# A transformer kernel whose second layer's keys and values are projected ahead of the experts and parked in DRAM

## The reference, cut to what matters

```
x = x + self_output(FFN(...(cross attention on layernorm(x) and ctx, then self attention)))   # 16 heads of 16
x = x + experts(layernorm(x))     # router of 8, top 2 of 7 experts and a no-op, 256 tokens an expert
x = x + mha(layernorm(x), ctx, ctx, W_q, b_q, W_k, b_k, W_v, b_v, W_o, b_o)                   # second layer
x = x + depth_block(layernorm(x)) # the better half of the tokens of a batch through one FFN
```

## Time and profile before

| What | Value |
|---|---|
| Median of 3 runs | 915.57 us (915.12 to 917.22) |
| Profiled execution, its own time | 916.68 us |
| Its span, first to last instruction | 914.9 us |
| TensorE busy | 779.9 us, 85% |
| VectorE busy | 563.6 us, 62% |
| ScalarE busy | 422.9 us, 46% |
| GpSimd busy | 394.8 us, 43% |
| DMA moved | 83.76 MB, mean 92 GB/s |
| Mean granted TensorE clock | 0.933 |

### The profile page before, as it was taken

How to read it: one execution, slowest core, us unless ns; L and a number is a source line. 1 busy time by engine, 2 the same in 40 slices (tenths; PEclk the granted TensorE clock), 3 DMA queues, 4 the chain that set the end, 5 groups by cost and what they waited for, 6 DMA issues and landing times.

```text
span 914.9 us, 16951 instructions
## 1 busy us (share of the span) xinstructions
PE 779.9 (85%) x6606; PEld 632.9 (69%) x6606; DVE 563.6 (62%) x1171; ACT 422.9 (46%) x703; POOL 394.8 (43%) x381
## 2 busy tenths in 40 slices
PE   4778999999999878999962999990677999779897
PEld 4655777777777646999862788880455767558896
DVE  4556887888878663779884002103568998855332
ACT  3134776777767566545610111210125677664132
POOL 7554573443455454635456220007845554242200
PEclk9978999999999999999985899995659999999999
DMA  8966677757785602300051551532775865500011
GB/s 195 173 119 95 118 122 101 107 91 130 115 123 97 82 3 93 117 1 26 27 204 44 180 200 39 89 115 65 129 125 83 117 99 72 71 3 12 13 35 35
DMA packets 58500, 83.76 MB, mean 92 GB/s; under 512 B 8722, under 2 KB 35345, under 8 KB 58372
## 3 DMA queue, kind: packets, MB, share of 16 engines
q1 hardware_dynamic: 55170, 76.47, 43.8%
q0 software_dynamic: 3072, 6.04, 2.8%
q10 hardware_dynamic: 178, 0.16, 0.1%
HBM read 36.74 MB, written 10.11 MB: 51 GB/s over the span
## 4 chain that ended last, share of the span: by engine, by line
PE 66%; DVE 13%; DMA 6%; POOL 5%; issue 4%; ACT 2%; SPq 2%; POOLq 0%; DVEq 0%; ACTq 0%
PE ps L608 8%; PE ps L187 8%; PE ps L672 7%; PE ps L188 6%; PE ps L189 6%; DVE nmax L1290 6%; PE ps L769 6%; PE ps L783 5%; PE ps L630 4%; PE ps L211 3%; PE ps L822 3%; PE ps L832 3%; PE ps L646 2%; POOL moe_in L1149 2%; DMA kst<-k_parts 2%
## 5 line engine op out<-in xcount | busy, mean ns | idle before, releaser
L1290 DVE TENSOR_REDUCE nmax<-ps 128x4 f32<-128x1024 f32 x192 | 234.9, 1224 | 93.2 <-PE ps L608 91.5
L915 ACT ACTIVATE prob<-ps 128x1024 f32<-128x1024 f32 x192 | 196.3, 1022 | 73.1 <-PE ps L630 71.1
L1074 POOL TENSOR_TENSOR rstd<-var,half 128x2 f32<-128x2 f32 x56 | 43.9, 784 | 279.4 <-DVE var L1241 202.3
L608 PE MATMUL ps<-kst,qst 50*128 50x256 f32 (+1 forms) x768 | 100.2, 343 | 32.8 <-DVE nmax L1290 22.6
L608 PEld LDWEIGHTS ps<-kst,qst 50*128 50x128 f32 (+1 forms) x768 | 60.6, 196 | 74.9 <-DVE nmax L1290 43.6
L672 PE MATMUL ps<-prob,vext 128*32 128x256 f32 x1536 | 106.9, 397 | 0.6 <-ACT oext L928 0.6
L630 PE MATMUL ps<-qst,kst 51*128 51x256 f32 (+1 forms) x768 | 81.5, 291 | 15.0 <-ACT prob L915 9.9
L630 PEld LDWEIGHTS ps<-qst,kst 51*128 51x128 f32 (+1 forms) x768 | 60.7, 192 | 21.7 <-ACT prob L915 13.3
L1161 POOL DMA_INDIRECT gat<-moe_out,slu x32 | 35.2, 1101 | 72.8 <-issue 72.8
L672 PEld LDWEIGHTS ps<-prob,vext 128*32 128x32 f32 x1536 | 41.2, 112 | 32.4 <-issue 4.2
L1082 POOL TENSOR_SCALAR hres<-xres,mv,rstd 128x256 f32<-128x256 f32 x48 | 58.9, 1232 | 2.6
(11 more groups left out here) (214 smaller groups left out, 2045.1 us busy)
## 6 DMA issues: line engine op xcount, KB each, us to landing
kst<-k_parts SPq DMA_DIRECT2D x144, 128.0 KB, 5.8
qst<-q_parts SPq DMA_DIRECT2D x144, 128.0 KB, 4.1
e_in<-in_ein SPq DMA_DIRECT2D x5, 1024.0 KB, 5.0
e_out<-in_eout SPq DMA_DIRECT2D x5, 1024.0 KB, 8.8
ctx_raw<-in_ctxT SPq DMA_DIRECT2D x16, 256.0 KB, 6.5
ew_in<-in_ein SPq DMA_DIRECT2D x2, 1024.0 KB, 6.2
ew_out<-in_eout SPq DMA_DIRECT2D x2, 1024.0 KB, 9.7
out<-xres SPq DMA_DIRECT2D x8, 256.0 KB, 2.1
```

Source lines behind the costliest of these rows:

```text
L608: last = pe.matmul(score_pair(n, p)[:, 512 * s + S * t:512 * s + S * (t + 1)], qst[j][a:b, p, t * P:(t + 1) * P], kst[j][a:b, p, :], start ...
L915: act.activation(probs[p % 4][:].rearrange("p i t s -> p (i t s)"), T_PS, ACT.Exp).then_inc(sm["exp_done"], 1)
L1290: dve.tensor_reduce(nmax[n % 2][:, :, :, p].rearrange("p t s -> p s t"), score_pair(n, p).rearrange("p (s t k) -> p s t k", s=2, t=TB), AX ...
```

## The change

K and V of all eight batches of the second layer are projected after the last FC2 and before expert 0 (`park` on TensorE). The contexts are loaded early in the FFN; ACT makes their rounded parts, VectorE the remainders. ACT writes K's rounded part out of PSUM; TensorE subtracts it in PSUM by a product with a negative identity, and ACT writes what is left as the remainder. V is copied out by ACT. Three DMAs per batch store both parts of K (512 KB) and V (256 KB) in DRAM; parts live in the buffers of the exponentials, so batches 4 to 7 wait for the stores of batches 0 to 3. Five DMAs per item (`stack_k`) bring them back later, K straight into the stack, V to a compact buffer (`vc`), from which POOL spreads it into vext (`values`).

The weights of W_k and W_v are split in the FFN (chunks 12 and 13), in buffers of their own. Experts use other buffers (E_BUF), and their first weights are loaded after FC2 of items 6 and 7. T_E0 is 2 later in the plan. In the entry, the combine of batch 1 stands a little later and that of batch 3 ahead of item 16's scores, batch 0's first tile is combined after two gathers, VectorE instead of POOL normalizes items 16 and 17, and the second half of the query stack of items 0 and 16, and of the key stack of item 0, is issued on ACT's queue. The three memsets of key stacks run after experts 2, 4 and 5 (before: 2, 3 and 6), those of vext on POOL. At the start the DMA of the zero mask comes later. Several semaphores are merged.

Core of the diff, sixteen leading blanks cut where there are as many. In order: constants and buffers; SP (park_load, park_store, stack_k, expert_weights, expert_tokens); TensorE's park; ACT's second_half and park and its wait before an expert's relu; POOL's values and attention; VectorE's second_stacks, queries, park and combine.

```diff
-T_E0 = T_F0 + F_STEP * (B - 1) + 54
+T_E0 = T_F0 + F_STEP * (B - 1) + 56
...
+    k_park = nc.dram_tensor("k_park", [B, 2, 2, P // 2, TB * S], F32, kind="Internal").ap()
+    v_park = nc.dram_tensor("v_park", [B, P, TB * D], F32, kind="Internal").ap()
...
-        SET = [n % 4 for n in range(12)] + [0, 1, 2, 0] + [n % 3 for n in range(NA, 3 * B)]
+        SET = [n % 4 for n in range(12)] + [0, 1, 2, 0] + [(n - NA) % 3 for n in range(NA, 3 * B)]
...
+        PARK_CTX = ((c_hi[1], c_lo[1]), (aT_hi, aT_lo),
+    *((t[0][:, 4 * i:4 * i + 2, :], t[0][:, 4 * i + 2:4 * i + 4, :]) for t in (qst, kst) for i in range(2)),
+    (hT_hi, hT_lo), (c_hi[0], c_lo[0]))
+        PARK_V = [vext[1 + i // 2][:].rearrange("p t h e -> p (t h e)")[:, i % 2 * TB * D:(i % 2 + 1) * TB * D] for i in range(4)]
...
+        PARK_K = (22.6, 24.4, 28.6, 32, 36.4, 38.9, 44, 46)
+        PARK_AT = dict(c_hi=(-77, -69, -64, -56, -51, -43, -4, 8.5), c_lo=(-76, -67.5, -63, -54.5, -50, -41.5, -2.5, 10.5))
+        PARK_STEP = dict(k=0, v=0.7, k_lo=1.5, k_hi=0.9, v_out=1.7, k_low=1.9, store=2.5)
...
-        E_BUF = [0, 3, 1, 2, 0, 3, 0]
+        E_BUF = [1, 2, 0, 3, 1, 2, 3]
...
+def park_load(b):
+    yield T_F0 + 5 if b < 4 else park_at(b - 4, "c_lo") + 2
+    if b == 0:
+        sp.wait_ge(sm["ctx_ready"], B)
+        sp.wait_ge(sm["oT_ps"], 2 * NA)
+    elif b == 2:
+        sp.wait_ge(sm["pv_ps"], 4 * NA)
+    elif b >= 4:
+        sp.wait_ge(sm["ctx_ready"], B + b - 3)
+    sp.dma_start(raw_ctx(b), ctxT[b].rearrange("(k p) s -> p k s", p=P)).then_inc(sm[ctx_sem(b)], 16)
+def park_store(b):
+    n = NA + b
+    yield park_at(b, "store") if b < 6 else T_E0 - 3.2 + 0.1 * b
+    sp.wait_ge(sm["k_split"], n + 1)
+    for c in range(2):
+        sp.dma_start(k_park[b, :, c], park_k(b)[:, c].bitcast(F32)).then_inc(sm[f"park{b % 4}"], 16)
+    sp.wait_ge(sm["park_s"], b + 1)
+    sp.dma_start(v_park[b], PARK_V[b % 4]).then_inc(sm[f"park{b % 4}"], 16)
...
+    if n >= NA:
+        yield expert_start((3, 5, 6)[n - NA]) + 4 if n < NA + 3 else start_of(n) - 6.7
+        if n < NA + NSET:
+            sp.wait_ge(sm["kst_one"], n - NA + 1)
+        else:
+            sp.wait_ge(sm["st_ps"], HG * (last_user(n) + 1))
+        if n == NA:
+            for i in range(4):
+                sp.wait_ge(sm[f"park{i}"], 96)
+            sp.wait_ge(sm["y_ready"], 1)
+        elif n >= NA + 2:
+            sp.wait_ge(sm["v_ready"], n - 1)
+        for s in range(2):
+            sp.dma_start(kst[j][64 * s:64 * s + 2 * DH].rearrange("p h s -> p (h s)").bitcast(F32),
+                         k_park[n - NA, s].rearrange("c (d q) x -> (c d) (q x)", q=4)).then_inc(sm[f"stk_k{j}"], 16)
+            sp.dma_start(kst[j][64 * s + 2 * DH:64 * s + 3 * DH].rearrange("p h s -> p (h s)").bitcast(F32),
+                         k_park[n - NA, s, 0].rearrange("(d q) x -> d (q x)", q=4)).then_inc(sm[f"stk_k{j}"], 16)
+        sp.dma_start(v_compact(n), v_park[n - NA]).then_inc(sm[f"stk_k{j}"], 16)
+        return
...
-    yield (T_F0 + 2, T_F0 + 10, ffn_start(7) + 13, ffn_start(7) + 27, *(expert_start(k) + 7.5 for k in (0, 1, 4)))[e]
-    if e == 0:
-        sp.wait_ge(sm["st_ps"], HG * NA)
-    elif e == 1:
-        sp.wait_ge(sm["op_ps"], NA)
+    yield (ffn_start(7) + 10, ffn_start(7) + 23, T_E0 - 2, T_E0 + 5.5, *(expert_start(k) + 7.5 for k in (1, 2, 3)))[e]
+    if e < 2:
+        sp.wait_ge(sm["fc2_ps"], B - 1 + e)
     elif e < 4:
-        sp.wait_ge(sm["fc2_ps"], e + 5)
-    else:
-        sp.wait_ge(sm["efc2_ps"], (0, 1, 4)[e - 4] + 1)
+        sp.wait_ge(sm["v_ps"], NA + B)
+    else:
+        sp.wait_ge(sm["efc2_ps"], e - 2)
...
-    yield expert_start(e) - (4 if e < 2 else 8)
+    yield expert_start(e) - 4 if e == 0 else expert_start(e) - 4.5 if e == 1 else expert_start(e) - 8
     if e == 0:
         sp.wait_ge(sm["scat"], 16 * 2 * NT)
         sp.wait_ge(sm["x_add"], B)
+        sp.wait_ge(sm["park_lo"], B)
...
+def park(b):
+    n, src = NA + b, PARK_CTX[b]
+    k_dst, v_dst = park_banks(b)
+    yield park_at(b, "k")
+    pe.wait_ge(sm["ctx_ready"], B + b + 1)
+    if b == 0:
+        pe.wait_ge(sm["w_lo_s"], 14)
+        pe.wait_ge(sm["gelu"], KF * B)
+    if b >= 2:
+        pe.wait_ge(sm["k_split"], n - 1)
+    for m in range(KD):
+        for k in range(KD):
+            last = mm3(pe, k_dst[m], [v[:, k, m * P:(m + 1) * P] for v in W[2][1]], [v[:, k, :] for v in src], k == 0, k == KD - 1)
+    last.then_inc(sm["k_ps"], 1)
+    yield park_at(b, "v")
+    if b == 2:
+        pe.wait_ge(sm["fres_s"], B)
+    elif b:
+        pe.wait_ge(sm["park_s"], max(b - 1, 1))
+    pe_project(pe, v_dst, W[2][2], src).then_inc(sm["v_ps"], 1)
+    yield park_at(b, "k_lo")
+    pe.wait_ge(sm["k_hi_s"], n + 1)
+    if b == 0:
+        pe.wait_ge(sm["nident_s"], 1)
+    for m in range(KD):
+        last = pe.matmul(k_dst[m], nident[:], park_k(b)[:, 0, m, :], start=False, stop=True, skip_group_check=True)
+    last.then_inc(sm["park_lo"], 1)
...
+def second_half(n, which, at):
+    yield at
+    act.wait_ge(sm[f"{which}_split"], n + 1)
+    if n:
+        act.wait_ge(sm["kst_one"], n - NA + 1)
+    else:
+        act.wait_ge(sm["init_d"], 2)
+    dst = (qst if which == "q" else kst)[SET[n]]
+    for c in range(3):
+        act.dma_start(dst[64 + DH * c:64 + DH * (c + 1), :, :].bitcast(F32), PARTS[which][c][64:128, :, :].bitcast(F32)).then_inc(sm[f"stk_{which}{SET[n]}"], 16)
...
+def park(b):
+    n = NA + b
+    yield park_at(b, "c_hi")
+    act.wait_ge(sm[ctx_sem(b)], 16 * (b // 4 + 1 + (0 if b % 4 else B)))
+    if b >= 6:
+        act.wait_ge(sm["fc1_ps"], KF // 2 * (b + 1))
+    elif b == 2:
+        act.wait_ge(sm["st_ps"], HG * NA)
+    elif b == 1:
+        act.wait_ge(sm["op_ps"], NA)
+    act.activation(PARK_CTX[b][0][:], raw_ctx(b), ACT.Copy).then_inc(sm["ctx_hi_s"], 1)
+    yield park_at(b, "k_hi")
+    act.wait_ge(sm["k_ps"], n + 1)
+    if b >= 4:
+        act.wait_ge(sm[f"park{b % 4}"], 48)
+    else:
+        act.wait_ge(sm["hid_ready"], 2 * (B - 1) + b // 2 * 2)
+    for m in range(KD):
+        last = act.activation(park_k(b)[:, 0, m, :], park_banks(b)[0][m], ACT.Identity, bias=cols[:, 5, m:m + 1])
+    last.then_inc(sm["k_hi_s"], 1)
+    yield park_at(b, "v_out")
+    act.wait_ge(sm["v_ps"], n + 1)
+    act.activation(PARK_V[b % 4], park_banks(b)[1], ACT.Copy).then_inc(sm["park_s"], 1)
+    yield park_at(b, "k_low")
+    act.wait_ge(sm["park_lo"], b + 1)
+    for m in range(KD):
+        last = act.activation(park_k(b)[:, 1, m, :], park_banks(b)[0][m], ACT.Identity, bias=cols[:, 5, m:m + 1])
+    last.then_inc(sm["k_split"], 1)
...
+            act.wait_ge(sm[f"park{2 * e + i}"], 96)
...
+def values(n):
+    j = n % VSET
+    if n < NA + VSET:
+        yield T_E0 + 15 + n - NA if j else T_C0 + 9
+        if j:
+            for i in range(2):
+                gp.wait_ge(sm[f"park{2 * (j - 1) + i}"], 96)
+        else:
+            gp.wait_ge(sm["st_y0"], 16 * 4)
+            gp.wait_ge(sm["st_y1"], 16 * 3)
+        ch(gp.memset(vext[j][:], 1.0))
+    yield T_E0 + 34 + 12 * (n - NA) if n < NA + 2 else start_of(n) + 2.5
+    gp.wait_ge(sm[f"stk_k{SET[n]}"], stk_k_count(n))
+    if n >= NA + VSET:
+        gp.wait_ge(sm["pv_ps"], 4 * (n - VSET + 1))
+    gp.tensor_copy(vext[j][:, :, :, 0:DH], v_compact(n).rearrange("p (t h d) -> p t h d", t=TB, d=DH)).then_inc(sm["v_ready"], 1)
...
-        power(0)
-        last = normed(hb(n), xb(n), 0)
-        last.then_inc(sm["xn_ready"], 1)
+        if n in (NA, NA + 1):
+            power(0, sm["x_pow"])
+        else:
+            power(0)
+            normed(hb(n), xb(n), 0).then_inc(sm["xn_ready"], 1)
...
-    for e, j in ((2, 1), (3, 2), (6, 0)):
+    for e, j in ((2, 0), (4, 1), (5, 2)):
...
+    if n in (NA, NA + 1):
+        yield t0 - (21 if n == NA else 17.2)
+        dve.wait_ge(sm["x_pow"], n - NA + 1)
+        for t in range(TB):
+            last = dve.tensor_scalar(hb(n)[:, t, :], xb(n)[:, t, :], mv[0][:, t, 0:1], rstd[0][:, t:t + 1], ALU.subtract, ALU.mult)
+        last.then_inc(sm["xn_ready"], 1)
     yield t0 - 12.4
     dve.wait_ge(sm["hT_hi_s"], n + 1)
     low(hT_hi, hT_lo, G[0]).then_inc(sm["hT_ready"], 1)
-    yield from split(n, "q", t0 - 9.4)
+    yield from split(n, "q", t0 - (5.6 if n == NA + 1 else 8.3 if n == NA + 2 else 9.4))
+def park(b):
+    yield park_at(b, "c_lo")
+    dve.wait_ge(sm["ctx_hi_s"], 2 + b)
+    hi, lo = PARK_CTX[b]
+    dve.tensor_tensor(lo[:], raw_ctx(b), hi[:].bitcast(F32), ALU.subtract).then_inc(sm["ctx_ready"], 1)
...
-    yield start_of(NA + b) - 23.4
-    dve.wait_ge(sm[f"gat_ld{b % 4}"], 64 * (b // 4 + 1))
+    at = T_C0 - (23.4, 12.3, 7.4, 4)[b] if b < 4 else start_of(NA + b) - 23.4
+    yield at
+    if b == 0:
+        dve.wait_ge(sm["gat_first"], 32)
+        dve.scalar_tensor_tensor(xres[:, 0, :], gat[:, 0, 0, 0, :], wsel[:, 0, 0:1], xres[:, 0, :], ALU.mult, ALU.add)
+    dve.wait_ge(sm[f"gat_ld{b % 4}"], 64 * (b // 4 + 1) - (0 if b % 4 else 32))
     for r in range(2):
         if r:
```

(12 more changed lines are left out.)

188 lines of the change are left out of this document (99 added, 89 removed).

## The result

The changed kernel takes 965.3 us (median of 4 runs, 957.6 to 968.0) against 916.0 for the kernel before: a ratio of 1.051, 95% interval 1.046 to 1.056. Forecast were 890.5 us and a range of 881 to 903. The profiled execution has a span of 962.8 us, 47.9 more than before.

The account below looks back on a forecast made before the run. TensorE was taken as busiest, VectorE next, both full in three second-attention periods; the chain of the tokens ends the hole. Terms -1.0 + 0.5 + 4.0 - 7.0 - 6.5 - 15.1 = -25.1 took 915.6 to 890.5 us, range 881 to 903.

Parts of the forecast that it names:

- I add 1.5 us for sharing: Hole: parking stores, weights and token load share SP's queue and DMA rate; 1.5 us of the +4.0 in sum.
- rival (d): Hole: parking stores at 107 GB/s bring expert 0 some 60 us late; time near 950 us; chance 0.05.
- The bounds of the term, 0 to +19: Hole: 0 if POOL hides the added work, +19 us if all 25 us of added matmuls become 44.
- rival (b): Hole: the lower clock holds, about +15 us instead of +4, and expert 0 stays cold (+1.4); 903 us; chance 0.10.
- each adds less than 1 us of new delay: Hole: batches 2 to 5, standing ahead of item 7's logits or routing counts, each add under 1 us.
- The projections: Experts: K and V of items 16 and 17 are no longer projected there, saving 5.6 us of the stage's -7.0.
- The POOL part: Entry: a key-stack memset moved into the experts gives -2.0 us, two normalizations moved from POOL to VectorE -2.1.
- Taken as -2.4: Entry: item 16's query DMAs, three on each of two queues, save three issues and some queueing, 2.4 us.
- taken 18.5: Second attention: the second period falls from 24.8 to 18.5 us, as item 18's K and Q leave single buffers.
- seven eighths: Second attention: some seven eighths of a period lie between item 23's stacks being allowed and landing; 14.1 us gives 16.5.
- rival (a): Second attention: VectorE and the stacking DMAs hold it, giving 7 us instead of 15.1; 898.6 us; chance 0.15.
- The FFN: FFN stage: added loads, copies, subtractions and weight splits cost 0 to 3 us, taken 0.5.

Follow-up runs that it names:

- e1: The changed kernel with each of a parked batch's two key stores split into two stores of 64 rows, same bytes: 922.7 us, ratio 1.0025.
- e3: e2 with the value store's destination given a slowest dimension of 2, and its load as two DMAs: 923.7 us.
- e2: e1 with the query stacks' first halves of items 17 and 18 issued at their place of before, behind the row maxima: 915.3 us, ratio 0.9969.
- e9: e2 without the parking stores of batches 4 to 7; items 20 to 23 load batches 0 to 3 instead: 912.8 us, ratio 0.9968.
- e7: e2 with parked batches 2 to 7 planned behind the logits of FFN item 7: 913.7 us, ratio 0.9952.
- e14: e10 with the batch order of e7: 919.0 us, ratio 1.0008.
- e10: e2 with all six stacking DMAs of item 16's queries issued by SP, none by ACT: 908.6 us, ratio 0.9881.
- e5: e2 with all parked batches planned later, behind the logits of items 6 and 7 and the routing counts: 917.4 us, ratio 0.9976.
- e13: e10 repeated without an edit, on the same chip as e12 and e14: 917.9 us, ratio 1.0000.
- e6: e2 with the parked key and value loads of items 19 to 23 left out: 910.5 us, ratio 0.9883.
- e12: e2 repeated without an edit, on the same chip as e13 and e14: 914.0 us, ratio 0.9943.

## Why the prediction was wrong

**The hole, the failed step.** It said "I add 1.5 us for sharing", and that the batches end near 501. That allowance was the only price of the parking stores; rival (d) judged them by 107 GB/s and by the 238 GB/s of two weight loads. Neither row has a destination like theirs. In the changed kernel a key store runs at 50 GB/s, a batch holds SP for 11 us, and expert 0 waits 20.75 us for a token load issued behind six of them: the hole grew by 42.8 us, 28.0 of which go with the shape (e1). Rival (d), given 0.05, named batches 4 to 7 behind the store four before, the threshold (the hole grows by over 29 us) and a time near 950; the token load behind the stores stood in the paragraph on the hole, without a price. Slow stores were the mechanism: e1 shows it by taking it out, e3 by putting some back. The bounds of the term, 0 to +19, came from the matmuls alone.

**The hole without the slow stores** (e1, e2, e9) is 49 us, +14.6 where +4.0 was forecast and +15 was rival (b). The clock is 0.80 there, and 0.75 from 470 to 500 (0.85 in the changed kernel), where above 0.9 was forecast; TensorE works 37.8 us. Item 7's transposes stand 16.5 us behind the last FC2 and not 11.5. With batches 2 and 3 behind them (e7, e14) it is 13.9: 2.6 of the 5.0 us are these two batches, a little more than "each adds less than 1 us of new delay", and 2.4 are batches 0 and 1, as forecast. Where the pause is missing (e10) the hole is 42.8 us, 6.3 shorter. The remaining 3.3 lie between item 7's logits and the last scatter (17.7 us in e10, 14.5 before). So +14.6 beside the +15 of rival (b) is in part luck: it had no pause in it, and what the lower clock costs no run separates. That another order wins them is not borne out: e5, e7 and e14 moved the batches, and their holes are 52.0, 48.9 and 48.6 us.

**Experts.** The projections were worth what was said: in e2 the stage is 5.4 us shorter (5.6 forecast), experts 15.2 us apart. Expert 0 gave nothing: its first half takes 8.88 us (under 8 forecast) behind 20.75 us of idling, and in e2, after 4.54 us of idling and at a clock of 0.76, 9.3. In the changed kernel 13.7 us came on top: TensorE idled 10.43 us for expert 1's tokens, whose load was issued at 558.54 behind the last stores, and expert 1's first half then took 10.22 us, at a clock of 0.70, where it takes 7.17 in e2.

**Entry.** The POOL part was right: TensorE waited 20.1 us for item 16's normalized tokens before, 15.8 now, -4.3 for a forecast of -4.1. "Taken as -2.4" for the landing failed: -0.4. A gather in the chain of the changed kernel, and the DMAs issued from 689 to 700 us by queue (issues, KB, us to landing):

```profile
692.97 6.68 DMA gat<-moe_out,slu
```

```profile
qst<-q_parts SPq DMA_DIRECT2D x3, 128.0 KB, 7.0
qst<-q_parts ACTq DMA_DIRECT2D x3, 128.0 KB, 6.0
gat<-moe_out,slu POOLq DMA_INDIRECT x4, 6.8
```

A stack took a median of 4.8 us to land before. Four gathers lay beside the stacks then too, so they alone don't explain the 6 to 7 us; the cause stays open. With one queue it is 18.1 to 18.4 us (e13, e10) for 17.1 before: the second queue makes up for what another part of the change costs here.

**Second attention.** -15.1 was forecast, -2.4 came, -5.3 with the order repaired. The step "taken 18.5" for item 17's period failed twice: the change's new stack numbers put item 18's queries ahead of item 16's maxima (26.1 us, which no part of the prediction saw), and even repaired it is 22.7, at a clock of 0.61. The last periods were taken as 16.5 and are 17.45. The Trainium skill (SBUF — State Buffer, "Door 1: The DMA port swizzle (why `[64,N]` ≈ `[32,N]`)") had given 17.0, which is nearer; but e6 shows 17.0 without any parked load, so the loads cost only 0.45 and no run here shows the rule to be the reason. The chain in e2 still ends at a parked load:

```profile
782.08 8.34 DMA vc<-v_park
```

Twelve DMAs became eleven, and the chain from the first query stack at 776.2 to the first scores at 790.5 takes 14.3 us; 14.1 was forecast. What failed is the conclusion from it to the period, for which the "seven eighths" were taken from the kernel before. The three periods in between took 57.7 us for 54.9, with VectorE at 49.7 and not at 51.8: at 86% it doesn't fill the periods any more. So of rival (a), whose -7 is near the -5.3, the half on VectorE is not borne out; that stacking DMAs hold the layer fits the chain above, but no run takes them out.

**Start and FFN.** The start gave 3.2 and not 1.0; in the other variants, whose code is the same up to there, item 15's first scores come at 311.2 to 315.1 us (316.2 before), so one trace says little on this term. The FFN took 1.7 of its 0 to 3 us more, above the 0.5 that was taken. Of the eight new subtractions on VectorE six take 0.68 us and two 1.77 and 1.73:

```profile
371.55 2.27 POOL L1249 TENSOR_TENSOR xres<-xres,rows 128x512 f32<-128x512 f32 x1
372.59 1.77 DVE L1444 TENSOR_TENSOR aT_lo<-oext,aT_hi 128x512 fp32r<-128x512 f32 x1
390.11 1.29 POOL L1249 TENSOR_TENSOR xres<-xres,rows 128x512 f32<-128x512 f32 x1
390.22 1.73 DVE L1444 TENSOR_TENSOR kst<-oext,kst 128x512 fp32r<-128x512 f32 x1
```

Both long ones begin while POOL adds two tensors and end 0.5 us behind it; one that began at 365.46, beside POOL's 128x2 power, took 0.68. The Trainium skill (SBUF — State Buffer, "SBUF: two separate sides") would have put the term at 3; the measured 1.7 lies in the middle. The two long ones fit the lock that it describes, and they are 2.1 us longer together than two of the short.

**Behind item 23** nothing was to change. In the changed kernel that stretch takes 5.4 us longer at a clock of 0.93; in e2 it takes 122.4 (122.6 before) at 0.98. In e10 it takes 127.9 us at 0.93, in e12 125.6 at 0.95: it goes with the clock of the profiled execution, and nothing shows that the change caused it.
